# Experts' loop: expert weight loads that wait for scatter-adds to land

## The reference

```
x = x + layernorm(mamba2(layernorm(x)))
t = layernorm(x)                                    # 8192 tokens of 256
shared = (silu(t @ Wg) * (t @ Wu)) @ Wd * sigmoid(t @ w)
w, idx = top_k(softmax(t @ gate_w), 8)              # of 64 experts
# every expert takes its first 128 tokens:
out_e = (silu(buf_e @ G_e) * (buf_e @ U_e)) @ D_e   # buf_e: 128 x 256
y[token] += weight * out_e[slot]
x = x + layernorm(y + shared)
```

## Time and profile before

| what | us or share |
|---|---|
| median of 3 runs | 1440.81 |
| the profiled execution's own time | 1442.88 |
| its span | 1441.2 |
| TensorE (PE) busy | 1234.0 (86%) |
| VectorE (DVE) busy | 1043.8 (72%) |
| ScalarE (ACT) busy | 929.1 (64%) |
| GpSimd (POOL) busy | 848.2 (59%) |
| SP's queue: expert gate and up loads, issue to landing (median) | 3.7 |
| POOL's queue: scatter-adds, issue to landing (median) | 4.8 |

### The profile page before, as it was taken

The page is one execution under the profiler, slowest core; times in us unless marked ns, Lnnn a source line. Parts: engine busy times, 40 slices in busy tenths (PEclk is TensorE's granted clock), DMA queues, the critical chain, the costliest instruction groups (busy, mean ns, idle before and its releaser), DMA issues. The chain is left out here.

```text
span 1441.2 us, 27240 instructions
## 1 busy us (share of the span) xinstructions
PE 1234.0 (86%) x8578; PEld 1073.9 (75%) x8578; DVE 1043.8 (72%) x3118; ACT 929.1 (64%) x2106; POOL 848.2 (59%) x1017
## 2 busy tenths in 40 slices
PE   2899999999999999999999999728989899998960
PEld 2677778777777877777777787528989888988960
DVE  3788989988998998998899899644443343443794
ACT  2677887787788778778878877543444344444453
POOL 0356556656655665665665566515666676664586
PEclk9899999999999999999999999958999999999985
DMA  5500011001001001100100000046666766765565
GB/s 164 184 1 30 25 34 40 24 26 38 31 24 38 33 24 33 38 24 24 40 31 24 25 32 17 31 134 183 167 152 166 175 163 161 176 153 113 176 201 176
DMA packets 112934, 119.90 MB, mean 83 GB/s; under 512 B 19888, under 2 KB 99056, under 8 KB 112880
## 3 DMA queue, kind: packets, MB, share of 16 engines
q1 hardware_dynamic: 97744, 94.58, 20.8%
q0 software_dynamic: 14336, 23.08, 8.5%
q10 hardware_dynamic: 800, 1.57, 0.3%
HBM read 70.63 MB, written 48.56 MB: 83 GB/s over the span
## 5 line engine op out<-in xcount | busy, mean ns | idle before, releaser
L1025 POOL TENSOR_TENSOR mamba_arena<-mamba_arena 128x512 f32<-128x512 f32 (+2 forms) x384 | 383.1, 1008 | 300.1 <-DVE mamba_arena L804 202.6
L454 PE MATMUL bank<-identity,mamba_arena 128*128 128x128 f32 x704 | 112.5, 279 | 53.0 <-DVE mamba_arena L913 27.5
L804 DVE TENSOR_TENSOR mamba_arena<-bank,mamba_arena 128x512 f32<-128x512 f32 (+1 forms) x224 | 136.3, 610 | 16.1 <-PE bank L498 7.6
L454 PEld LDWEIGHTS bank<-identity,mamba_arena 128*128 128x128 f32 x704 | 85.0, 146 | 80.1 <-issue 27.3
L1370 PE MATMUL bank<-xt_hi,wsgu_hi 128*128 128x256 f32 x384 | 114.0, 297 | 17.1 <-DVE xt_lo L1753 13.8
L1370 PE MATMUL bank<-xt_lo,wsgu_hi 128*128 128x256 f32 x384 | 109.6, 285 | 0.0
L1370 PE MATMUL bank<-xt_hi,wsgu_lo 128*128 128x256 f32 x384 | 109.6, 285 | 0.0
L662 ACT ACTIVATE mamba_arena<-bank 128x512 f32<-128x512 f32 x192 | 100.3, 539 | 10.1 <-PE bank L454 7.6
L804 DVE TENSOR_TENSOR mamba_arena<-mamba_arena 128x512 f32<-128x512 f32 (+1 forms) x128 | 54.6, 427 | 49.0 <-ACT mamba_arena L662 46.8
L1370 PEld LDWEIGHTS bank<-xt_hi,wsgu_hi 128*128 128x128 f32 x384 | 74.6, 194 | 18.7 <-DVE xt_lo L1753 14.4
L666 ACT ACTIVATE mamba_arena<-x_all,mamba_arena 128x256 f32 (+1 forms) x128 | 69.9, 595 | 21.5 <-DVE mamba_arena L850 15.4
(11 more groups left out here) (367 smaller groups left out, 4496.0 us busy)
## 6 DMA issues: line engine op xcount, KB each, us to landing
experts_arena<-in_egu SPq DMA_DIRECT2D x64, 256.0 KB, 3.7
routed_sum<-zeros SPq DMA_DIRECT2D x1, 8320.0 KB, 27.0
x_all<-in_x SPq DMA_DIRECT2D x32, 256.0 KB, 2.7
token_table<-mamba_arena SPq DMA_DIRECT2D x64, 128.0 KB, 1.7
normed_transposed<-mamba_arena SPq DMA_DIRECT2D x32, 256.0 KB, 2.0
experts_arena<-normed_transposed SPq DMA_DIRECT2D x32, 256.0 KB, 3.8
experts_arena<-in_edown SPq DMA_DIRECT2D x64, 128.0 KB, 2.9
experts_arena<-routed_sum SPq DMA_DIRECT2D x32, 256.0 KB, 3.5
```

The source lines that it names most:

```text
L454: return nc.tensor.transpose(out, in_, identity[:, :])
L804: return nc.vector.tensor_tensor(out, a, b, op)
L1025: return nc.gpsimd.tensor_tensor(out, a, b, op)
```

## The change

Four waits are added to SP's queue in each pass. The first of unit 1's gate and up loads, and with it the m tile's load, waits until the scatter-add `added00` of step j1 - 1 has landed; the second one until `added01` of that step has. The first of unit 0's loads waits until `added10` of step j0 - 2 has landed; the second one until `added11` has. No line is moved: the m tile's load keeps its place in the queue, and the first wait stands ahead of it. The waits on `added00` and `added01` are guarded by `real(j1 - 1, 16)` alone, those on `added10` and `added11` by `real(j0, 16)` too. The diff, with the waits and what stands around them:

```diff
                         eng.dma_start(xt[:, 0]..., xnt_d[j0]...).then_inc(xt_loaded, 16)
+                    if real(j1 - 1, 16):
+                        eng.wait_ge(added00, 16 * j1)
                     if not odd and real(d, 8):
                         if real(d - 1, 8):
                             eng.wait_ge(m_xt_split, d)
...
                         eng.dma_start(wgu[:, 1, 0], egu_d[4 * j1 + 2]...).then_inc(wgu_loaded10, 16)
+                    if real(j1 - 1, 16):
+                        eng.wait_ge(added01, 16 * j1)
                     if real(j1, 16):
                         eng.dma_start(wgu[:, 1, 1], egu_d[4 * j1 + 3]...).then_inc(wgu_loaded11, 16)
...
                         eng.dma_start(wdown[:, 1, 0, :], edown_d[4 * j1 + 2]...).then_inc(wdown_loaded10, 16)
+                    if real(j0 - 2, 16) and real(j0, 16):
+                        eng.wait_ge(added10, 16 * j0 - 16)
                     if real(j0, 16):
                         if real(j0 - 1, 16):
                             eng.wait_ge(up_e_done0, j0)
                         eng.dma_start(wgu[:, 0, 1], egu_d[4 * j0 + 1]...).then_inc(wgu_loaded01, 16)
+                    if real(j0 - 2, 16) and real(j0, 16):
+                        eng.wait_ge(added11, 16 * j0 - 16)
                     if real(j0, 16):
                         eng.dma_start(wgu[:, 0, 0], egu_d[4 * j0 + 0]...).then_inc(wgu_loaded00, 16)
```

## The result

| | before | after |
|---|---|---|
| median of 4 runs, us | 1440.60 (1439.72 to 1441.05) | 1456.62 (1454.13 to 1458.38) |
| ratio | | 1.0119, 95% interval 1.0096 to 1.0142 |
| the profiled execution, its span | 1442.88, 1441.2 | 1454.13, 1452.4 |

The change makes the kernel slower by 16.0 us; 1444.2 was forecast, with 1453 as the upper end of the range.

What follows compares the result with a forecast made beforehand. It took the chain of scatter-adds, each waiting for the previous landing, to bound the loop, TensorE next. Loop -8.6 and end +12.0 made +3.4 us, so 1444.2 against the median 1440.81; range 1430 to 1453, its own 1436 to 1451.

Steps and rivals of the forecast that it cites:

- Four waits that bind, and where the loads go: SP's queue: all four waits hold SP; loads follow landings by 0.3 us, the first at -0.45 from the next scatter-add's start.
- s11 at 4.7, s01 at 4.9: Loop: scatter-adds counted by added11 and added01 take 4.7 and 4.9 us to the next start.
- Taken: 6.0: Loop: the scatter-add counted by added00 meets the long load train and takes 6.0 us, bounds 5.15 to 7.3.
- s10 at 5.1: Loop: the scatter-add counted by added10 meets 256 + 128 + 128 KB and takes 5.1 us, from 4.84 to 5.34.
- 8.6 us less: Loop: steps of 20.8 us instead of 21.46, 0.66 us less each, save 8.6 us in 13 steps.
- The end, 12.0 dearer: Loop's end: last-pass waits delay the tail's loads; TensorE's tail starts 9.5 us later, slow clock adds 2.5: 12.0 us.
- the slow clock: TensorE's tail: after longer idleness it runs at a granted clock of 0.50 for 5 us, costing some 2.5 us.
- The lateness of loads costs nothing in the loop: Loop: expert loads issued later still arrive before TensorE needs them, with 4 us left; cost nothing.
- rival 3: Loop: loads come late, TensorE waits 1 us for weights in each of 13 steps: 1466 us; chance 0.05.
- the second: Loop: contention only changes place, a step stays at 21.46 us, the end costs 12.0: 1452.8 us; chance 0.21.
- The first: Loop: spreading works fully, TensorE sets a step of 19.7 us, 22.5 less, end 12.0 more: 1430.3 us; chance 0.21.
- three signs of being wrong: Loop and tail: steps under 20.3 us, a tail within 15 us of its scatter-add, or TensorE waiting for expert weights.

Runs made afterwards that it cites:

- The fourth release alone: Guarded kernel, but SP's wait on added11 becomes waits for a POOL no-op and then its own 64-byte store's landing: 1428.70 us, ratio 0.9935.
- guarded kernel: The changed kernel without its first two waits (added00, added01) in the last pass, where no load follows them: 1445.67 us, ratio 1.0063.
- all four early releases: Guarded kernel, same load order, but all four landing waits become waits for a POOL no-op and then a 64-byte store's landing: 1425.27 us, ratio 0.9902.

## Why the prediction was wrong

The direction held and the size did not. Step by step:

- **Four waits that bind, and where the loads go: right.** Forecast was -0.45, +0.1, +0.7, +1.25, with the store up to +1.85, around s00; the queue has -0.59, +0.02, +0.62, +1.17, +1.82.
- **s11 at 4.7, s01 at 4.9: right** (4.67, 4.88).
- **"Taken: 6.0" for s00: wrong, and this is the step that failed.** It measured 6.81, in the upper half of the bounds 5.15 to 7.3, and makes 10.5 us of the 12.3 by which 13 steps missed. The row that I took, the s11 of 1186.84, had loads from 1186.07 to 1187.87, so -0.77 to +1.03; I called its train the same with 256 KB more in front, wrote that its late loads stand just where s11's stood, and passed over that they stand later now, up to +1.8. The fourth release alone, which starts the same train some 1.4 us earlier (its first load at -2.01, its last at +0.09 below, in a step without the store), brought s00 from 6.81 (guarded kernel) to 5.63, and all four early releases brought it to 5.33. So place, with the order and bytes kept, is the larger part of its price above POOL's 4.7: 1.2 of 2.1 us with the fourth release alone, 1.5 with all four. POOL and SP in the kernel with the fourth release alone:

```profile
1200.20 1.62 POOL L2000 DMA_INDIRECT routed_sum<-experts_arena,scatter_now  x1 [0.53 <-issue]
...
1205.54 1.62 POOL L2016 DMA_INDIRECT routed_sum<-experts_arena,scatter_now  x1 [1.16 <-DVE gather_now L1820]
```

```profile
1198.19 0.40 SPq L1309 DMA_DIRECT2D experts_arena<-in_egu  x1
...
1200.29 0.33 SPq L1270 DMA_DIRECT2D experts_arena<-normed_transposed  x1
```

- **s10 at 5.1: too low by 0.28** (5.38). With s00's 0.81 and the smaller differences, 0.94 us a step against the 20.8 of the sum, or 12.3 us in 13 steps. "8.6 us less" became 3.7 more.
- **The end, 12.0 dearer: right** (11.0). The tail started 9.6 later (22.87 - 13.28), 9.5 forecast; the slow clock cost 1.47 (13.25 - 11.78), 2.5 forecast, as it lasted 3.4 us and not 5. (The forecast's own rows give 2.2: 23 matmuls that take 2.8 us at the rate of 96 in 11.78 took 5.0.)
- **The lateness of loads costs nothing in the loop: right.** TensorE is idle 1.69 us a step before and 1.56 after (278.94 - 256.91 and 282.64 - 262.30, over 13), and every gap over 0.2 us ends where it turns gathered token rows (L1363 before, L1371 after), none in a matmul on expert weights; rival 3, for which TensorE would wait 1 us more, is out. In the tail the late load cost what was forecast. The rule to issue a DMA early and to wait for it late (the Trainium skill, "DMA: Bandwidth & Descriptors", Rules for kernel authors) agrees with the trace there; in the loop the trace shows no price for being late.
- **TensorE's clock in the loop: not in the sum, and not what made the steps longer.** TensorE is busy 5.4 us more in the 13 steps of after (262.30 against 256.91) for 2052 matmuls against 2053, as the granted clock, 1.00 in the other steps, averages 0.92 or 0.93 in five of them (one before), each time behind a gap of 2.2 to 2.7 us in its work; one such gap had no fall behind it. These five take 21.81 us in the mean, the other eight 21.70; the guarded kernel has two such steps and the same s00 of 6.81.
- **The rivals.** Nearest is the second: the contention changed its place, and a step that stays at 21.46 with an end of 12.0 made 1452.8; the step even grew by 0.28. The first, in which most of s00's train is through before its rows move, did not come about here. Its step is reached by the early releases (19.84, 19.7 forecast for it), though s00 has 5.33 there and not 5.15. None of the three signs of being wrong that the prediction named came: steps under 20.3, a tail within 15 us of its s10, TensorE waiting for expert weights.

On the profiled executions +3.4 was forecast and +11.2 seen: 12.3 more from the steps, 1.0 less from the end, 0.5 more from the last full step, 4.0 less from where the loop starts. The 4.0 is luck: it hid a part of the miss. The medians differ by 4.8 us more than the profiled executions do; which stage that is in, no single trace shows.

Why a load behind the start slows a scatter-add's landing is left open: the runs show the place and the price, not the resource that the two share.

## What to carry to other kernels

When a chain of transfers bounds a loop, price a load beside it by its issue time against the transfer's start, and take the price from a row with the same offsets: here a train that reached 0.8 us further behind the start, with 256 KB more in front, cost 1 us more (6.81 for s00 after, 5.85 for s11 before), and the same train let go 1.4 us earlier 1.2 us less. To spread loads, release them from something that comes well ahead of the next transfer (here 2.0 to 2.7 us behind the last one's start); a landing, here, released them 0.6 us ahead of the transfer that they disturbed. Before a wait is put into an in-order queue, look what stands behind it in the last pass, where its own load no longer exists: that was 8 to 12 of the 16 us here.

## What was not expected of the hardware

- A no-op on POOL behind an indirect DMA, with a semaphore to raise, was not held back by the gather ahead of it in the queue: the load that it released went 0.62 us behind the start of the scatter-add and 1.31 us ahead of the gather (1164.63 against 1164.01 and 1165.94).
- A small transfer late in a scatter-add still goes with a slow landing: with 16 instead of 128 rows in the last load, at +1.51, s01 came 6.00 us behind s00, where loads at -0.60 and +0.35 alone gave 4.93. How much of it belongs to the down load at +0.93, these runs do not separate.
- A 64-byte store and the wait for its landing held SP for 1.43 us (1154.67 to 1156.10). That is not a steady delay: over fourteen passes the fourth release's takes 1.11 to 2.31 us in that kernel, and 1.14 to 2.55 in the one with the fourth release alone.
- TensorE's clock came back to 1.00 some 3.4 us after it resumed in the tail, behind 10.7 us of idleness; ahead of the loop, behind 13.7 us, it was 0.50 for at least 5 us of work.
